# Both 16-head attentions of width 16: a new order of TensorE's work in rounds of two pairs of heads

## The reference, cut to what matters

```python
q, k, v = split_heads(x @ Wq + bq), split_heads(ctx @ Wk + bk), split_heads(ctx @ Wv + bv)
scores = einsum('bhqd,bhkd->bhqk', q, k) / 4
attn = softmax(scores)                    # grouped: a mask is added first,
                                          # and attn is multiplied by group_prob after
out = einsum('bhqk,bhkd->bhqd', attn, v) @ Wo + bo
```

## Time and profile before

| | us |
|---|---|
| median of 3 runs | 1496.47 |
| lowest, highest | 1486.98, 1496.73 |
| the profiled execution | 1487.34 |
| its span | 1485.6 |

### The profile page before, as it was taken

The page is one execution under the profiler, slowest core; times in us unless marked ns, Lnnn a source line. Parts: engine busy times, 40 slices in busy tenths (PEclk is TensorE's granted clock), DMA queues, the critical chain, the costliest instruction groups (busy, mean ns, idle before and its releaser), DMA issues. The chain is left out here.

```text
span 1485.6 us, 25339 instructions
## 1 busy us (share of the span) xinstructions
PE 1190.9 (80%) x9507; PEld 952.7 (64%) x9507; DVE 887.7 (60%) x1940; ACT 682.9 (46%) x1499; POOL 515.5 (35%) x505
## 2 busy tenths in 40 slices
PE   2999999999987777489996399999994479996143
PEld 2777777777763454367775398888884357774032
DVE  6665456455433436657776466666662667776586
ACT  3444543555432111356664154555540266664643
POOL 3465554555541000588876321111003341100211
PEclk9999999999998998679998599999998689998555
DMA  5000000000001420301102345555531200002100
GB/s 169 11 1 11 12 11 1 11 1 2 1 1 22 134 62 15 83 21 41 40 12 88 129 156 173 197 184 181 178 110 56 82 22 23 12 2 75 29 0 25
DMA packets 59814, 88.60 MB, mean 60 GB/s; under 512 B 8528, under 2 KB 49696, under 8 KB 59696
## 3 DMA queue, kind: packets, MB, share of 16 engines
q1 hardware_dynamic: 57584, 81.49, 17.9%
q0 software_dynamic: 2112, 5.51, 1.2%
HBM read 81.48 MB, written 5.51 MB: 59 GB/s over the span
## 5 line engine op out<-in xcount | busy, mean ns | idle before, releaser
L872 POOL TENSOR_SCALAR a_arena<-a_arena 112x487 f32<-112x487 f32 x128 | 192.9, 1519 | 175.1 <-DVE a_arena L1082 175.1
L1160 ACT ACTIVATE a_arena<-banks,a_arena 112x487 f32<-112x487 f32 x128 | 84.3, 664 | 191.4 <-DVE a_arena L1076 191.4
L1076 DVE TENSOR_REDUCE a_arena<-banks 112x2 f32<-112x974 f32 x64 | 75.0, 1172 | 105.1 <-PE banks L962 105.1
L103 PE MATMUL banks<-f_x_high,f_up_high 128*128 128x256 f32 x448 | 129.0, 288 | 3.6 <-DVE f_up_low L1927 2.2
L104 PE MATMUL banks<-f_x_low,f_up_high 128*128 128x256 f32 x448 | 128.3, 286 | 0.0
L105 PE MATMUL banks<-f_x_high,f_up_low 128*128 128x256 f32 x448 | 128.2, 286 | 0.0
L366 POOL TENSOR_TENSOR a_arena<-a_arena 112x375 f32<-112x375 f32 x128 | 114.3, 921 | 20.0 <-ACT a_arena L680 19.6
L103 PE MATMUL banks<-a_kvT_high,a_wk_high 128*128 128x488 f32 (+1 forms) x192 | 82.8, 431 | 46.8 <-DVE a_wk_low L578 42.9
L480 PE MATMUL banks<-ident,a_arena 112*126 112x112 f32 x768 | 105.9, 275 | 14.4 <-POOL a_arena L366 12.7
L480 PEld LDWEIGHTS banks<-ident,a_arena 112*126 112x126 f32 x768 | 77.8, 144 | 48.2 <-issue 27.2
L1964 POOL DMA_INDIRECT f_arena<-f_rows,f_arena x28 | 32.1, 1148 | 199.7 <-PE banks L1997 178.3
(11 more groups left out here) (333 smaller groups left out, 3336.3 us busy)
## 6 DMA issues: line engine op xcount, KB each, us to landing
f_arena<-in_L_ffn_w1T SPq DMA_DIRECT2D x15, 1024.0 KB, 6.1
f_arena<-in_L_ffn_w2T SPq DMA_DIRECT2D x15, 1024.0 KB, 9.7
f_arena<-in_L_ffn_w3T SPq DMA_DIRECT2D x14, 1024.0 KB, 5.0
a_arena<-in_ctxT SPq DMA_DIRECT2D x24, 375.0 KB, 4.8
a_arena<-in_ctx SPq DMA_DIRECT2D x16, 375.0 KB
f_y<-f_arena SPq DMA_DIRECT2D x14, 256.0 KB, 5.5
a_arena<-in_L_xattn_Wkv SPq DMA_DIRECT2D x2, 1024.0 KB, 9.8
a_arena<-in_fside_BxSxS SPq DMA_DIRECT2D x8, 164.1 KB, 2.5
```

Of the source, the lines that this page charges most:

```text
L103: pe.matmul(out, sh, mh, start=start, stop=False)
L872: pool.tensor_scalar(z, z, inv[:, n % 4, s:s + 1], None, ALU.mult).then_inc(p_ready, 1)
L1076: dve.tensor_reduce(negmax[:, n % 4, :], banks[0:T, 0:2, 0:KEYS], AX, ALU.max, negate=True).then_inc(max_ready, 1)
L1160: act.activation(prob[n % PR][s][:, 0:KEYS], banks[0:T, s, 0:KEYS], ACT.Exp, bias=negmax[:, n % 4, s:s + 1], accum_out=total[:, n % 4, s:s ...
```

## The change

TensorE's loop now goes in rounds of two pairs, n even: S(n+2) and S(n+3) together, T(n), W(n/2 - 1), T(n+1), and then the pieces of n and of n+1, one behind the other. W for pairs n-2 and n-1 now stands in the round of n, between its two transposes. VectorE's loop becomes maximum(n+2), copy_turned(n), and the rest as before; ScalarE's becomes copy_turned(n), exponent(n+2), and the rest as before. The table of pieces, the banks, the waits inside the steps, and GpSimd's and SyncE's loops stay.

```diff
--- before.py
+++ after.py
@@ -522,16 +522,20 @@
             scores(0)
             pe.wait_ge(x_low, 4)
             scores(1)
-            for n in range(LAST):
-                if n + 2 < PAIRS:
-                    scores(n + 2)
+            for n in range(0, LAST, 2):
+                for k in (n + 2, n + 3):
+                    if k < PAIRS:
+                        scores(k)
                 if n < PAIRS:
                     turn(n)
-                if n >= 3 and n % 2 and n < PAIRS + 2:
-                    weigh((n - 3) // 2)
-                if n in later:
-                    bank_free(n)
-                    piece(later[n], 7)
+                if 2 <= n < PAIRS + 2:
+                    weigh(n // 2 - 1)
+                if n < PAIRS:
+                    turn(n + 1)
+                for k in (n, n + 1):
+                    if k in later:
+                        bank_free(k)
+                        piece(later[k], 7)
 
         @block.vector
         def _(dve):
@@ -641,11 +645,12 @@
             for j in range(4, 8):
                 evacuate(first[j], first_bank[j])
             maximum(0)
+            maximum(1)
             for n in range(LAST + 1):
-                if n + 1 < PAIRS:
-                    maximum(n + 1)
-                if 0 < n <= PAIRS:
-                    copy_turned(n - 1)
+                if n + 2 < PAIRS:
+                    maximum(n + 2)
+                if n < PAIRS:
+                    copy_turned(n)
                 if n >= 4 and n % 4 == 0 and n <= PAIRS:
                     invert(n // 4 - 1)
                 if n >= 6 and n % 4 == 2 and n <= PAIRS + 2:
@@ -718,11 +723,13 @@
                 for e in range(2):
                     act.activation(qm[0][:, c, e, f * HALF:(f + 1) * HALF], q_parts[j % 2][0][:].bitcast(F32),
                                    ACT.Copy, scale=qmask[:, e:e + 1]).then_inc(qm_high, 1)
+            exponent(0)
+            exponent(1)
             for n in range(LAST + 1):
                 if n < PAIRS:
-                    exponent(n)
-                if 0 < n <= PAIRS:
-                    copy_turned(n - 1)
+                    copy_turned(n)
+                if n + 2 < PAIRS:
+                    exponent(n + 2)
                 if n >= 6 and n % 4 == 2 and n <= PAIRS + 2:
                     spread(n // 4 - 1)
                 if n % STEPS == 4 and n // STEPS + 2 < B:
```

## The result

The changed kernel takes 1676.11 us (median of 4 runs, 1675.03 to 1679.30) beside 1493.96 us for the kernel before (1486.98 to 1496.73). The ratio is 1.1232 with a 95% interval of 1.120 to 1.1265: slower, as forecast, and 39 us less slow than the forecast of 1715. The span grew from 1485.6 to 1673.8 us, by 188. In what follows the times of loops are spans of profiled executions, measured from the first to the last W (L499) of each loop, and a batch is the time from one I piece (L434) to the next but one.

A forecast was written before the change was run, and what follows sets the result against it. TensorE was taken to bound both loops. 1487.3 us plus 155 for waits at full clock, net of the paired scores' saving, made 1642; plus 75 for a lower clock, 1717, given as 1715, range 1600 to 1800.

The forecast's parts named there:

- TensorE bounds the loops, the others have slack: Both loops before: TensorE busy 161 to 162 of 165 us, the other engines less.
- The paired scores cost one S: Two S together on all four row groups take 0.70 us instead of 1.4.
- the saving of 37 us: TensorE's own work in both loops: about 0.6 us per round, 2.3 per batch, 37 over 16 batches.
- The program-order rule of the Trainium skill: Matmuls start and end strictly in program order; by it each round some 0.4 us longer, 26 us in all.
- That this gains only where TensorE remains the bound: Condition on the whole gain; the rival where it holds and pairing pays in full: 1450 us, chance 0.03.
- W behind move_out: Rounds with n mod 4 = 2: W waits for move_out of the sum before, starting at 3.8 instead of 1.4 us.
- The pieces in bank 7: Second piece waits for the first's evacuation; bare costs K0 to K1 1.26 + 0.1, V0 to V1 0.76 + 0.1, O to I 0.5 + 0.1.
- T behind expand: Grouped loop, n mod 4 = 0: T(n+1) waits for T(n), copy, invert, expand and regroup, starting at 4.9 us.
- The full-clock sum, +155: Both loops at full clock: 8.6 us more per plain batch, 11.2 per grouped, eight each, less about 4; 1642 us.
- The clock, +75, half of 150: TensorE's clock falls in the loops' holes; bounds 0 and +150 us, half taken. Rivals: clock holds 0.26, low throughout 0.12.
- One sign: Expected in the profile after: both loops at 220 to 260 us instead of 165.
- The hole at 913: One idle TensorE microsecond in the trace, soon followed by three fully busy ones at clock 0.50; evidence for a falling clock.

The follow-up runs named there:

- the experiment: Kernel after with spread and move_out at the head of their steps, plus invert ahead of copy_turned(n) on VectorE: 1578.23 us, ratio 1.0603.
- e1_early_out: Kernel after with spread and move_out at the head of their steps on ScalarE and VectorE: 1570.45 us, ratio 1.0536.
- e11_tensor_only: Kernel after with VectorE's and ScalarE's orders put back to those of the kernel before: 1554.94 us, ratio 1.0423.
- e5_scores_paired: Kernel before with S(n+2) and S(n+3) taken together at even n, in both loops: 1498.47 us, ratio 1.0063.
- e4_fill: Kernel after with 24 dense matmuls on constant data (the filling) before W where n mod 4 = 2, results unused: 1710.52 us, ratio 1.1494.
- e7_orders_only: Kernel before with the new orders of VectorE and ScalarE alone, TensorE's order as it was: 1743.88 us, ratio 1.1701.

## Why the prediction was right, point by point

*TensorE bounds the loops, the others have slack.* Right: the three other engines did the same work in a grouped loop 76% longer (274.5 / 155.7).

*The paired scores cost one S.* Right where the second pair's banks are free: four wide at 1418.17, 0.72 us to the next transposes. In the plain loop that failed in 11 of 31 rounds, and the saving of 37 us had not allowed for it. The program-order rule of the Trainium skill ("TensorE: Matmul & The Clock Gate", Part 3), which would have made each round some 0.4 us longer, does not hold here: four first matmuls of two pairs lie in one row of 0.44 us before and 0.45 us after, as long as the row of one pair's two (0.42 to 0.43).

*That this gains only where TensorE remains the bound.* Right in kind, but I had not asked at which wait the pair itself stops. Alone it gains in the grouped loop and loses in the plain one.

*W behind move_out.* Right. Forecast W 2.4 us late; the round shown has 2.0 (2.7 instead of 0.7), the others 1.8 to 2.4, and the mean idle time over 30 rounds is 1.8 (53.9 / 30). Taking it away gave 106 us, more than its own time.

*The pieces in bank 7.* Right: K1 waited 1.3 us, V1 0.8, I 0.6, as the bare costs say.

*T behind expand.* Right for the kernel after: TensorE waited for regroup, 35.9 us in the grouped loop, and T(n+1) starts 4.5 us behind the first S of its round (778.39 to 782.91), where I had 4.9. Wrong about what would cure it: the experiment left invert behind the reduction and expand ahead of the regroup, and gained nothing.

*The full-clock sum, +155.* Too high. One part is the number of batches: I took eight full ones and gave back 4 us for the ends. Between the first and the last I there are seven, of which the last is a short one, and outside them the loops hardly grew. From I to I, the seven batches of each loop grew by 116 and 71 us, 187 in all, which is the whole change. Also the batch of before was 20.7 us, not 20.4 and 20.5: the mean over 14 intervals had the short last one in it. The other part is the length of a batch: 28.4 us, with filling, is an upper bound for a plain batch at full clock, where I had 29.0. The grouped loop came at 37.6 us, 0.67 to 0.69 of the clock, so my 31.7 at full clock was not seen; the nearest is one grouped batch with filling, 32.5 us at 0.93. With 31.7 and 28.4, seven batches each, less 20.7, make 7 x 11.0 + 7 x 7.7 = 131 us, an upper estimate.

*The clock, +75, half of 150.* By difference 188 - 131 leaves about 57 us. A second estimate comes from TensorE's busy time: the 230 matmuls of a batch take 19.0 us at full clock (e1_early_out plain, e11_tensor_only grouped) and 26.5 (grouped) and 22.1 to 23.6 (plain) in the kernel after, some 80 us more over all fourteen batches. In e1_early_out the 1.5 us between a batch at 0.93 and one at 1.00 is all busy time; were it so here, the clock would make about 80 us and the waits about 110. So the clock cost some 57 to 80 us, inside the bounds 0 and 150, and more in the grouped loop (0.70) than in the plain one (0.85), which I had not told apart. The rows before did not decide between the bounds, and that half came so near is luck. What is shown without an estimate is that same-code batches differ by 1.5 us between 0.93 and 1.00, and that removing one wait returned twice its time.

Together: forecast 1487 + 155 + 75 = 1717; measured 1487 + 188 = 1675, of which 110 to 131 is waits and the rest the clock. One sign failed: I had both loops at 220 to 260 us, and the grouped one took 274.5 (plain 228.0). The hole at 913 that I called one microsecond was 1.76 us long (idle before 914.47), so it is a little shorter than the 2.3 us worked out for the loops, and longer than the shortest of 1.4.

## What to carry to other kernels

Where TensorE is the bound, read each wait in its new order before counting what it saves: for every instruction moved, ask what the engine that frees its bank must do first. Work that closes a group (here spread and move_out) belongs at the head of the other engines' steps, as early as its inputs allow. An instruction moved ahead of one neighbour gains little if another that waits still stands before it, as the reduction before invert. One edit can gain in one variant of a function and lose in another; ask for each which instruction frees the bank.

## What the runs showed of the hardware that was not expected

Scores of two pairs on disjoint 32-row groups run four wide although the second pair's six matmuls stand behind all six of the first in the program: 0.78 us for the twelve, once ahead of each loop before, and 0.72 us to the next transposes inside the loops of the kernel after and in the grouped loop of e5_scores_paired.

24 dense 128x128x128 matmuls took 2.8 us at full clock, 0.12 us from one to the next, as much as the 0.12 us of a V piece's 256 columns; half the columns did not halve the time (e4_fill).

Short holes can hold the mean clock of a whole loop low. In e7_orders_only, where no wait of TensorE in the grouped loop was longer than 2.3 us, it was busy for 84% of 309 us at a mean clock of 0.55, 2.4 GHz being 1.00 and 1.2 GHz 0.50, while the kernel before, with the same matmuls and 98% busy, had 0.99. A lower clock makes the engine look busier, so busy time is to be read with the clock beside it.
